# Decoder layer on one core: the end of batch 0's attention and the start of its cross-attention placed further ahead in the head loop, with the search steps that go with them

## What is computed

```
x = _layernorm(x + _L0_attn_ref(x, ...))          # 16 heads of 128, 4-bit weights x scales, softmax over 512 keys
x = _layernorm(x + _L0_xattn_ref(x, ..., 54))     # one head of width 512 over 1024 context rows, top 54 scores kept
x = _layernorm(x + _L0_ffn_ref(x, ...))           # silu(gate) * up, inner width 2048
```

```
scores = coef * einsum('bsd,bnd->bsn', Q, ctx); scores -= max
thr = top_k(scores, 54)[0][..., -1:]
att = softmax(where(scores < thr, -inf, scores))
```

## Time and profile before

| | |
|---|---|
| median of 3 runs | 941.55 us (941.02 to 942.08) |
| the profiled execution, its time | 941.75 us |
| its span | 940.0 us |
| PE busy | 913.1 us, 97% |
| DVE busy | 593.0 us, 63% |
| ACT busy | 575.3 us, 61% |
| POOL busy | 491.5 us, 52% |

### The profile page before, as it was taken

One profiled execution on the slowest core, in us unless ns is written; L12 is line 12 of the kernel. 1 busy time (PEld: TensorE's weight loads), 2 busy tenths in 40 slices (PEclk: granted clock), 3 DMA queues, 4 the chain that ended last, 5 costly groups with the idle time before them and its releaser, 6 DMA issues.

```text
span 940.0 us, 13220 instructions
## 1 busy us (share of the span) xinstructions
PE 913.1 (97%) x4440; PEld 750.9 (80%) x4440; DVE 593.0 (63%) x1066; ACT 575.3 (61%) x1142; POOL 491.5 (52%) x407
## 2 busy tenths in 40 slices
PE   9999999999999999999989989899999999999997
PEld 7788788887788877887768778798888888888885
DVE  5666966678666776667694899974878225411114
ACT  4767876688766878787875466543664635443333
POOL 4257652646626467376744457644674751354440
PEclk9999999999999999999999999999999999999999
DMA  6532230122301222123112202332433341343321
GB/s 203 157 92 67 74 101 1 50 69 74 102 1 35 84 72 74 58 57 96 40 56 90 91 23 91 90 101 68 126 120 102 101 123 34 112 125 91 99 80 45
DMA packets 46102, 76.97 MB, mean 82 GB/s; under 512 B 5584, under 2 KB 11216, under 8 KB 45776
## 3 DMA queue, kind: packets, MB, share of 16 engines
q1 hardware_dynamic: 45600, 75.68, 27.5%
q10 hardware_dynamic: 432, 0.39, 0.2%
HBM read 73.69 MB, written 2.36 MB: 81 GB/s over the span
## 4 chain that ended last, share of the span: by engine, by line
PE 41%; DVE 7%; ACT 2%; issue 2%; POOL 0%; ACTq 0%; DVEq 0%; POOLq 0%
PE p L895 6%; PE p L896 6%; PE p L899 6%; PE p L909 3%; PE p L911 3%; PE p L910 3%; PE p L861 2%; PE p L862 2%; PE p L863 2%; DVE m L1561 1%; PE p L776 1%; PE p L773 1%; PE p L774 1%; DVE acc L1522 1%; PE p L876 1%
## 5 line engine op out<-in xcount | busy, mean ns | idle before, releaser
L1496 DVE TENSOR_SCALAR_CACHE_REDUCE JK<-p,ssc 128x512 bf16<-128x512 f32 x112 | 83.7, 748 | 113.0 <-PE p L660 113.0
L1983 POOL TENSOR_TENSOR V<-RAW,V 128x512 fp32r<-128x512 f32 x64 | 82.4, 1311 | 134.1 <-ACT V L1075 134.1
L1021 ACT ACTIVATE PR<-p,nms,ssc 128x512 f32<-128x512 f32 x112 | 87.4, 781 | 60.1 <-DVE JK L1496 58.7
L2068 POOL TENSOR_TENSOR acc<-SX,acc 128x512 f32<-128x512 f32 x54 | 69.8, 1292 | 74.7 <-ACT SX L1055 51.5
L678 PE MATMUL p<-R 128*128 128x512 f32 x248 | 97.3, 392 | 0.8 <-DVE V L1489 0.8
L1983 POOL TENSOR_TENSOR C<-RAW,C 128x512 fp32r<-128x512 f32 x58 | 76.1, 1325 | 39.9 <-ACT C L1075 39.9
L1813 DVE TENSOR_TENSOR SX<-p,SX 128x512 f32<-128x512 f32 x32 | 22.1, 692 | 109.0 <-PE p L899 99.7
L1509 DVE TENSOR_TENSOR PT<-p,PT 128x512 fp32r<-128x512 f32 x128 | 87.5, 684 | 5.2 <-ACT PT L1040 5.1
L713 PEld LDWEIGHTS p<-ident,PR 128*128 128x128 f32 x512 | 62.4, 140 | 21.2 <-DVE PT L1509 6.6
L713 PE MATMUL p<-ident,PR 128*128 128x128 f32 x512 | 77.4, 274 | 1.0
L1040 ACT ACTIVATE PT<-p 128x512 fp32r<-128x512 f32 x128 | 75.8, 592 | 0.7 <-PE p L713 0.7
(11 more groups left out here) (243 smaller groups left out, 2740.1 us busy)
## 6 DMA issues: line engine op xcount, KB each, us to landing
RAW<-in_wg SPq DMA_DIRECT2D x32, 256.0 KB, 2.8
RAW<-in_wu SPq DMA_DIRECT2D x32, 256.0 KB, 2.7
RAW<-in_ctxn SPq DMA_DIRECT2D x32, 256.0 KB, 2.8
RAW<-in_wd SPq DMA_DIRECT2D x32, 256.0 KB, 2.8
RAW<-in_wq SPq DMA_DIRECT2D x19, 256.0 KB, 2.7
RAW<-in_wk SPq DMA_DIRECT2D x18, 256.0 KB, 2.8
RAW<-in_wv SPq DMA_DIRECT2D x16, 256.0 KB, 2.8
RAW<-in_wo SPq DMA_DIRECT2D x16, 256.0 KB, 4.9
```

Source lines behind the costliest of these rows:

```text
L1021: e.activation(PR[:, i % 2, :], P[i % 2][:, :], ACT.Exp, bias=nms[:, i % 4:i % 4 + 1], scale=ssc[:, 0:1] if HB[j][0] > 1 else SC, accum_ou ...
L1496: e.tensor_scalar(JK[:, :], P[i % 2][:, :], ssc[:, 1:2] if HB[i // 4][0] > 1 else -SC, None, ALU.mult, ALU.min, accum_out=nms[:, i % 4:i % ...
L1983: e.tensor_tensor(lo, RAW[:, slot[key], :], hi, ALU.subtract).then_inc(*c_lo.up(key))
L2068: e.tensor_tensor(acc[:, r], OBUF[:, (4 * q + tt) % 2], acc[:, r], ALU.add).then_inc(*rows[r].up((q, 1)))
```

## The change

The last output tiles of batch 0 (`q` = 13, rows 2 and 3) move from quarters 118 and 119 to 116 and 117, `borow` from 114 to 113. The projections of pair 31 move from quarters 120 and 121 to 119 and 120, and their weights' loads and splits one quarter ahead too. The norm of batch 0 moves one to two quarters ahead, its transposed rows from 121 and 122 to 119 and 120, the query products from 123 and 124 to 121 and 122, the first cross scores from 125 to 123, the second ones from 126 to 125. The context tiles of batch 0 are loaded and converted one quarter earlier, and a score product now waits for the one context tile that it reads, no longer for all eight. Search steps: two in each of the quarters 124 to 127 (before: 1, 2 and 2 in 125 to 127), and the three steps ahead of the last additions go.

The diff, cut to its core; the ring plan, ACT, DVE and POOL follow the tensor program's moves:

```diff
 def o_tile(i):
     j, qt = divmod(i, 4)
+    if j == 29:
+        return (13, 2 + qt) if qt < 2 else None
     return (j // 2 - 1, 2 * (j % 2) + qt - 2) if qt >= 2 and j >= 2 else None
+
+def qk_tile(i):
+    j, qt = divmod(i, 4)
+    if i in (119, 120):
+        return 31, i - 119
+    return (j + 1, qt) if qt < 2 and j + 1 < NJ - 1 else None
...
-    if qt in (1, 2) and j + 3 < NJ and WJ[j + 3] == j + 3:
-        out.append(("qk", j + 3, qt - 1))
+    a = qt if j == 28 else qt - 1
+    if a in (0, 1) and j + 3 < NJ and WJ[j + 3] == j + 3:
+        out.append(("qk", j + 3, a))
...
+XSAT = (123, 125)
...
         def x_scores(n, hf, k):
-                w.wait_ge(*c_lo.at(("ct", b, 7)))
                 ps = claim(k, xs_out, (n, hf))[:, :]
                 for m in range(4):
+                    w.wait_ge(*c_lo.at(("ct", b, 2 * m + hf)))
                     w.wait_ge(*qx_hi.at((b, m)))
...
@@ def tensor @@
-                if qt < 2 and j + 1 < NJ:
-                    proj_qk(j + 1, qt)
+                if qk_tile(i):
+                    proj_qk(*qk_tile(i))
...
-                if i == 114:
+                if i == 113:
                     ps = claim(BANK["borow",], borow, 0)
...
-                if j == 30 and qt in (1, 2):
-                    for r in (2 * qt - 2, 2 * qt - 1):
+                if i in (119, 120):
+                    for r in (2 * (i - 119), 2 * (i - 119) + 1):
                         ps = claim(BANK["x2t", r], x2_lo_d, r)
...
-                if i in (123, 124):
-                    for m in (2 * (i - 123), 2 * (i - 123) + 1):
+                if i in (121, 122):
+                    for m in (2 * (i - 121), 2 * (i - 121) + 1):
                         q_proj(0, m, BANK["qx", m])
-                if i in (125, 126):
+                if i in XSAT:
+                    n = XSAT.index(i)
                     for hf in range(2):
-                        x_scores(i - 125, hf, BANK["xs", i - 125, hf])
+                        x_scores(n, hf, BANK["xs", n, hf])
...
@@ def vector @@
-                if (j, qt) == (29, 3):
+                if i == 118:
                     ln_stats(1, [2, 3], row_writers(2)[-6])
                     ln_rstd(1, 0, 4)
-                if j == 30 and qt < 2:
-                    for r in (2 * qt, 2 * qt + 1):
+                if i in (118, 119):
+                    for r in (2 * (i - 118), 2 * (i - 118) + 1):
                         ln_apply(1, r, 0)
...
-                if i in (125, 126):
+                if i == 124:
                     topk.ready.add(0)
-                    search(topk.run(i - 124))
-                if i == 127:
+                if i >= 124:
+                    search(topk.run(2))
+                if i == 126:
                     topk.ready.add(1)
-                    search(topk.run(2))
             search(topk.run(1))
             topk.ready.add(2)
             search(topk.run(1))
             ot_low(NJ - 1)
-            search(topk.run(3))
             for tt in range(4):
                 o_add(NJ // 2 - 1, tt, 0)
...
@@ def gpsimd @@
-                if 115 <= i <= 122:
-                    add_bias(i - 115, "bo2")
+                if 114 <= i <= 121:
+                    add_bias((2, 3, 0, 1, 4, 5, 6, 7)[i - 114], "bo2")
-                if 122 <= i <= 124:
-                    for n in range(3 * (i - 122), min(3 * (i - 121), 8)):
+                if 121 <= i <= 123:
+                    for n in range(3 * (i - 121), min(3 * (i - 120), 8)):
                         conv_ct(0, n)
```

More of the change, by code:

```diff
@@ L224, in ring_plan @@
         j, qt = divmod(i, 4)
-        if qt < 2 and j + 1 < NJ:
-            take("qk", j + 1, qt)
+        if qk_tile(i):
+            take("qk", *qk_tile(i))
         if qt == 0 and j > 0:
@@ L1209, in scalar @@
                 j, qt = divmod(i, 4)
-                if qt < 2 and j + 1 < NJ:
-                    qk_high(j + 1, qt)
+                if qk_tile(i):
+                    qk_high(*qk_tile(i))
                 if qt == 3:
@@ L1697, in vector @@
                     maximum(i + 2)
-                if qt < 2 and j + 1 < NJ:
-                    qk_low(j + 1, qt)
+                if qk_tile(i):
+                    qk_low(*qk_tile(i))
                 if qt == 3:
```

59 lines of the change are left out of this document (30 added, 29 removed).

## The result

The changed kernel takes 954.17 us (median of 4 runs, 953.05 to 955.52), the kernel before 941.28 (940.53 to 942.08): a ratio of 1.0135, 95% interval 1.0123 to 1.0146. The profiled execution took 954.18 us, the one before 941.75, so it stands at the median.

What follows compares the result with a forecast made beforehand. DVE's queue bounds from 530 to 607 us, PE ahead of and behind it. At tile 3's mask 7.8 + 3.5 - 1.3 = 10.0 us later: profiled 941.75 becomes 951.75, so 951.5 us; range 944.5 to 955.5.

Steps and rivals of the forecast that it cites:

- PE's waits: PE up to the end of `scores(126)`: waits of 9.8 us against 5.0 before, 4.8 more.
- Bank: Pair 30's second projection on PE waits 1.6 us until DVE has read the bank of the first one.
- keys: The third matmul of `scores(120)` waits 0.7 us for the low part of pair 30's keys.
- norm: PE waits 4.75 us for the first normed row of batch 0, where it waited 1.34 before.
- context tile: First cross scores: PE waits 1.75 us for context tile 6, converted on ACT, then POOL.
- Clock at the norm: Behind the 4.75 us wait for the first normed row, PE's granted clock falls to half, costing 1.8 us.
- rival (3): Last output tiles: no 1.93 us wait or half clock, 3.9 us gained, tile 3's mask not binding; 937.6 us, chance 0.07.
- DVE up to `OT`: DVE needs 19.7 us from `scores(126)` to the last `OT`; first statistics of rows 4 and 5 come 7.8 us later.
- The strands: Search on DVE: three steps removed are paid again ahead of tile 3's mask, 3.5 us, less 1.3 of vanished waits.
- Behind the mask: Behind tile 3's mask PE is the bound again, with no cover of size; next waits some 0.5 us each.
- Rival (2): The half clock also follows PE's waits of 1.6 and 1.75 us: 3.6 us more, 955.1 us, chance 0.12.
- Rival (4): The table load's drain shows ahead of the root, first norm 1.4 us later: 952.9 us, chance 0.04.

Runs made afterwards that it cites:

- before_tiles_moved: The kernel before with only the change's moved output tiles and projections, and what goes with them; 944.72 us, ratio 1.0029.
- after_fill_norm: The changed kernel with 16 unread matmuls in PE's wait ahead of the first normed row; 951.64 us, ratio 1.0107.
- after_old_search: The changed kernel with the search steps where the kernel before has them; 952.21 us, ratio 1.0116.
- before_new_search: The kernel before with only the change's search steps, everything on PE where it was; 944.84 us, ratio 1.0035.
- before_in_step: The kernel before with the search strands in step up to tile 3, the even one five steps ahead from tile 4 on; 941.64 us, ratio 0.9996.
- before_fill_mask: The kernel before with ten unread matmuls ahead of the transpositions of tile 3's mask; 941.92 us, ratio 0.9999.
- before_in_step_convert_first: The kernel before, search strands in step, three context tiles converted by ACT and POOL ahead of tile 2's transposed mask; 942.14 us, ratio 1.0001.
- after_in_step: The changed kernel with the search strands in step up to tile 3, the even one five steps ahead from tile 4 on; 949.28 us, ratio 1.0074.
- after_fill_in_step: The changed kernel with 16 unread matmuls ahead of the first normed row and strands in step up to tile 3; 946.89 us, ratio 1.0055.

## Why the prediction was right, step by step

**PE's waits.** Right in place and order. Bank 1.6 (measured 1.60), keys 0.7 (0.60), norm 4.75 (4.19), query products 0.85 (0.77), context tile 1.75 (1.56). The sum of 9.8 was 1.1 too high. What it was set against was further off: of the "5.0 us" that the prediction called waits of before, the trace shows 2.53 as waits. The rest are small gaps between matmuls of different kinds, which stay. So PE got 6.2 us of waits more, not 4.8. With the clock's 2.3 that makes 8.5, and the same work takes 8.0 us more (460.79 to 522.40, against 53.58); the gaps too small for the list are 0.5 us less. `before_tiles_moved` shows the first two by themselves.

**Clock at the norm.** The fall was right; its price was 1.8 in the sum and is 2.3 by the rows with and without it (2.5 by the times of `after_fill_norm`). It was priced from eight matmuls at the last output tiles, and here it held for eight transpositions and a projection. (The prediction's 3.9 us for the old place of the half clock is 1.93 and 1.8, so 3.7; rival (3) alone rests on it.) Waits and clock together put `scores(126)` at 521.3 instead of 520.1.

**DVE up to `OT`.** 19.7 us predicted, 19.7 measured. PE's wait for `OT`, 2.5 predicted, was 1.72, and the half clock that should have followed did not come. The first statistics, predicted 7.8 us later, are 7.85 later: the 1.2 of the start and the absent half clock cancel. That number was right by luck in its parts.

**The strands.** The step on which the forecast turned holds: the moved steps buy nothing for tile 3's mask. Shown by three kernels: the search part alone costs 3.3 us, putting it back gives 2.0, and keeping the strands in step gives 4.9 at an otherwise unchanged kernel. The distance from the statistics to the mask goes by the order of the steps in every kernel here: 68.2 us in the kernel before, `after_old_search` and `before_tiles_moved`, 72.5 in the changed kernel and `before_new_search`, 66.1 with the strands in step. The term was mis-sized, 2.2 in the sum and 4.3 in the trace. The search's steps in the stretch, 46 instead of 43, take 3.9 us more, where 3.5 were counted. Of the credit of 1.3 for waits that vanish only 0.6 came: DVE's idle time from the statistics to the mask is 2.02 before and 1.44 after, as the wait of 0.71 went and the one of 0.61 is 0.74 now. And the three maskings ahead of the last take 5.5 us instead of 4.8, a term that the prediction did not have: POOL's conversions fall on other maskings (see the run with the conversions moved).

**Behind the mask.** The prediction had PE as the bound with no cover of size, and nothing was given back. It missed 0.6 us for the half clock, and it missed POOL's conversions as a second bound 1.7 us behind the first, which takes the gain from two experiments and which in the changed kernel only hides most of the half clock.

In sum: forecast +10.0, measured +12.4 in the profiled executions, +12.9 in the medians. The excess of 2.1 at the mask and 0.6 behind it, less 0.3 later on, is the difference. Rival (2), half clock behind the waits of 1.6 and 1.56, gave nearly the right time for a wrong reason: behind those the granted clock stayed at 1.00. The range reached up to 955.5 only because of that rival, so that it holds the measured 954.2 is luck as well; the forecast's own time was 2.7 us short. Rival (4) did not occur: the root starts 1.29 us behind the start of the table load in the changed kernel too (480.51 and 481.80).

## What to carry to other kernels

Work that is moved ahead leaves a hole where it stood and shortens the cover of what it passed: ask for each moved piece what it hid. When two chains take turns, count the steps ahead of the one result that is waited for, not the steps removed, and then look for the next result of the same kind, or the gain is given back there. Before a stretch at half clock is counted as loss, look for what would wait in it at full clock. And where one execution runs ahead of another, compare distances within each, not clock readings between them.

## What the runs showed of the hardware

The granted clock went from 1.00 to 0.50 in or behind waits of PE of 1.93, 2.49, 2.66, 4.19, 4.83 and 6.94 us, and stayed at 1.00 behind those of 1.56, 1.60 and 1.72 us. The length does not decide: 2.11 us (`before_tiles_moved`) left it at 1.00, while one of 2.05 in `before_in_step` and, in one execution, one of 1.71 (`before_fill_mask`) were followed by 0.50, and in `before_in_step_convert_first` it fell behind one of 1.21 that followed one of 2.05. The same wait of 2.04 us ahead of tile 2's mask left it at 1.00 in `after_in_step` and was followed by 0.50 in `after_fill_in_step`. Behind the wait of 2.91 us for tile 3's mask the eight transpositions took 1.86 us at 0.50 in the kernel before, and 1.06 at 1.00 in `before_tiles_moved` and `after_old_search`, where the clock fell only behind them. What decides was not found. It was back at 1.00 some 5 us behind the end of the wait at the norm (482.95 to 488), 7 at tile 3's mask before (606.84 to 613.6), and 9 there in the changed kernel (618.96 to 628).

Filling a wait with matmuls that nobody reads made the kernel faster by 2.5 us. Of the two places tried it was worth it where the wait was long (4.19 us), the bank was free at once, and what followed was PE's own work.

A masking product on DVE (`SCALAR_TENSOR_TENSOR`, 128x1024, in float32) that began while POOL was in the middle of an instruction took 1.08 us more than what was left of it, 1.27 to 2.32 us in 60 cases; with POOL idle it took 1.27 to 1.29 (52 cases). Other kinds of instructions on DVE were not compared.
